# Two attention stages and the last scatters of a four-layer model: DRAM row for the spread, products for the last group, adds into the output

## The reference, cut to what matters

```python
# L1 and L3 attention, per head of 64 columns
attn = softmax(q @ k.T * scale)        # 1024 queries; 1024 + 154 keys
out  = (attn @ v) @ Wo + bo

# L3 feed-forward: 32 experts, 4 chosen of each of 2048 tokens, 320 places in each expert
buf_tok = full(E * cap + 1, N).at[dest].set(tok)     # a free place holds the token number N
out = einsum(silu(xe @ w1) * (xe @ w3), w2) * buf_w
y = zeros((N + 1, DIM)).at[buf_tok].add(out)[:N]     # what falls on row N is dropped
return y + z                                         # z is a shared expert
```

## Time and profile before

| | us |
|---|---|
| median of 3 runs | 3202.24 (3200.54 to 3202.68) |
| the profiled execution's own time | 3204.76 |
| its span, first to last instruction | 3203.0 |
| PE busy in the span | 2851.1 (89%) |
| DVE busy | 1890.4 (59%) |
| ACT busy | 1432.0 (45%) |
| POOL busy | 586.9 (18%) |

### The profile page before, as it was taken

How to read it: one execution, slowest core, us unless ns; L and a number is a source line. 1 busy time by engine, 2 the same in 40 slices (tenths; PEclk the granted TensorE clock), 3 DMA queues, 4 the chain that set the end, 5 groups by cost and what they waited for, 6 DMA issues and landing times. The chain is left out here.

```text
span 3203.0 us, 46363 instructions
## 1 busy us (share of the span) xinstructions
PE 2851.1 (89%) x13988; PEld 2126.9 (66%) x13989; DVE 1890.4 (59%) x3602; ACT 1432.0 (45%) x2987; POOL 586.9 (18%) x655
## 2 busy tenths in 40 slices
PE   5796779986997989999689999999999999968996
PEld 4795545546886779999456666666666666646665
DVE  4414465516555354443588888878788888664443
ACT  1233544431211224544347766767676777711111
POOL 0133010001442200000200000000000000106776
PEclk8698879996999779999799999999999999979999
DMA  1342022223232010000112323233222332335776
GB/s 40 107 163 92 1 32 23 22 11 117 84 103 81 13 40 27 26 13 1 24 25 24 31 22 31 22 33 31 31 21 30 23 31 22 13 72 149 162 173 144
DMA packets 153723, 168.84 MB, mean 53 GB/s; under 512 B 38128, under 2 KB 123014, under 8 KB 153286
## 3 DMA queue, kind: packets, MB, share of 16 engines
q1 hardware_dynamic: 115878, 105.16, 20.2%
q0 software_dynamic: 21280, 37.93, 5.5%
q10 hardware_dynamic: 16416, 24.12, 2.3%
HBM read 105.77 MB, written 29.84 MB: 42 GB/s over the span
## 5 line engine op out<-in xcount | busy, mean ns | idle before, releaser
L2036 ACT ACTIVATE l3a_pt_hi<-l3a_banks 128x512 fp32r<-128x512 f32 (+2 forms) x640 | 382.9, 598 | 326.6 <-PE l3a_banks L1977 272.4
L2147 DVE TENSOR_TENSOR l3a_pt_lo<-l3a_pt,l3a_pt_hi 128x512 fp32r<-128x512 f32 (+2 forms) x640 | 459.9, 727 | 75.9 <-ACT l3a_pt L2037 38.8
L2037 ACT ACTIVATE l3a_pt<-l3a_banks 128x512 f32<-128x512 f32 (+2 forms) x640 | 378.7, 592 | 0.0
L2117 DVE TENSOR_REDUCE l3a_maxima<-l3a_banks 128x1 f32<-128x1178 f32 x256 | 351.5, 1375 | 3.5 <-PE l3a_banks L1924 3.3
L2182 POOL TENSOR_TENSOR l3a_out_t<-l3a_out,l3a_shared 64x512 f32<-64x512 f32 x65 | 90.3, 1390 | 1134.2 <-DMA l3a_shared<-l3a_inverse 1134.2
L1977 PE MATMUL l3a_banks<-l3a_pt_hi,l3a_v 128*65 128x512 f32 (+2 forms) x640 | 287.7, 449 | 6.1 <-ACT l3a_out L2051 3.8
L1990 PE MATMUL l3a_banks<-l3a_q,l3a_k 128*128 128x512 f32 (+2 forms) x640 | 253.9, 397 | 13.0 <-ACT l3a_pt L2037 11.4
L1991 PE MATMUL l3a_banks<-l3a_q,l3a_k 72*128 72x512 f32 (+5 forms) x640 | 252.8, 395 | 0.0
L1977 PE MATMUL l3a_banks<-l3a_pt_lo,l3a_v 128*65 128x512 f32 (+2 forms) x640 | 251.9, 394 | 0.0
L1977 PE MATMUL l3a_banks<-l3a_pt_hi,l3a_v_lo 128*65 128x512 f32 (+2 forms) x640 | 251.8, 393 | 0.0
L1924 PE MATMUL l3a_banks<-l3a_k,l3a_q 128*128 128x512 f32 (+1 forms) x768 | 207.3, 378 | 16.0 <-DVE l3a_maxima L2117 16.0
(11 more groups left out here) (583 smaller groups left out, 5876.7 us busy)
## 6 DMA issues: line engine op xcount, KB each, us to landing
l3f_w<-in_L_ffn_w SPq DMA_DIRECT2D x96, 256.0 KB, 3.7
l0f_w<-in_L_ffn_W ACTq DMA_DIRECT2D x12, 1024.0 KB, 6.5
l1f_w<-in_L_ffn_W ACTq DMA_DIRECT2D x18, 512.0 KB, 4.6
l3a_shared<-l3a_inverse SPq DMA_DIRECT2D x65, 128.0 KB, 6.3
l2f_w<-in_L_ffn_w SPq DMA_DIRECT2D x16, 512.0 KB, 4.5
l3a_q<-l3a_q SPq DMA_DIRECT2D x64, 128.0 KB, 2.3
l3a_k<-l3a_k SPq DMA_DIRECT2D x64, 128.0 KB, 2.3
l0f_w<-in_L_ffn_W SPq DMA_DIRECT2D x4, 1024.0 KB, 7.2
```

Of the source, the lines that this page charges most:

```text
L2036: act.activation(a.pt_hi[0:rows, n % a.pt_slots, :], a.st_bank[0:rows, n % 2, :], ACT.Exp, bias=bias, scale=scale)
L2037: act.activation(a.pt[0:rows, n % 4, :], a.st_bank[0:rows, n % 2, :], ACT.Exp, bias=bias, scale=scale).then_inc(a.exped, 1)
L2117: dve.tensor_reduce(a.maxima[:, n:n + 1], banks.rearrange("p a b -> p (a b)")[:, 0:KEYS], AX.X, ALU.max).then_inc(a.maxed, 1)
L2147: dve.tensor_tensor(a.pt_lo[0:rows, slot, :], a.pt[0:rows, n % 4, :], a.pt_hi[0:rows, slot, :].bitcast(F32), ALU.subtract).then_inc(a.lo_m ...
```

## The change

- `inverse` is no longer a row in SBUF but a DRAM tensor of 512 floats. The inverted totals are written to it (128 partitions with 16 bytes each), and the spread reads it 64 times from DRAM.
- The last group of the last unit no longer goes over SP and POOL. PE turns its row of totals by four products with one row and one column ("tr": 1x128 by 1x1) into 128x4; DVE inverts them, multiplies them with the identity matrix into `diagonal` (128 x 512); one product with ones ("ts": 128x128 by 128x512, float32) puts every inverted total on every partition; DVE multiplies `out` with it out of PSUM into `out_t`. Then "e4" to "e7" follow as before.
- The scatters of the last feed-forward part add to the output tensor itself, with a bound: indices over 2047 are dropped. The rows of zeros behind the tokens and the copy at the end are gone.

```diff
-        self.inverse = sb("inverse", [1, BLOCK])
+        self.inverse = nc.dram_tensor("l3a_inverse" if projected else "l1a_inverse", [1, BLOCK], F32, kind="Internal").ap()
+        self.diagonal, self.last_totals = sb("diagonal", [P, BLOCK]), sb("last_totals", [P, BLOCK // P])
@@ side_pe
+    elif name == "tr":
+        pe.wait_ge(a.o_kept, number(unit, GROUPS - 1) + 1)
+        for n in range(BLOCK // P):
+            ins = pe.matmul(bank[:, n:n + 1], a.out[HEAD:HEAD + 1, 1, n * P:(n + 1) * P], chip.ones[HEAD:HEAD + 1, 0:1], start=True, stop=True)
+    elif name == "ts":
+        pe.wait_ge(a.diagonal_made, 1)
+        ins = pe.matmul(bank[:], chip.ones[:], a.diagonal[:], start=True, stop=True)
...
-            pe.wait_ge(a.ot_done, number(unit, 1 if t == 0 else 3) + 3)
+            pe.wait_ge(a.ot_done, number(unit, 1 if t == 0 else 2) + 3)
+            if t == 4:
+                pe.wait_ge(a.side_read[uses.bank("ts")], uses.read_with("ts"))
@@ move_totals
-    sp.dma_start(a.inverse[:], a.totals[:]).then_inc(a.returned, 16)
+    sp.dma_start(a.inverse.rearrange("a (p n) -> (a p) n", p=P), a.totals[:]).then_inc(a.returned, 16)
     sp.wait_ge(a.returned, k * 16 + 16)
-    sp.dma_start(a.shared[:, g % 2, :], a.inverse[:].unsqueeze(1).to_broadcast([1, HEAD, BLOCK])).then_inc(a.spread_out[g % 2], 16)
+    sp.dma_start(a.shared[:, g % 2, :], a.inverse.rearrange("a n -> (a n)").partition_broadcast(HEAD)).then_inc(a.spread_out[g % 2], 16)
@@ in place of attention_end
+def attention_end_pe(pe, chip, a, last, project):
+    for name in ("tr", "ts", *OWN_LAST):
+        side_pe(pe, chip, a, a.epilogue(last), name, last, 1, project)
+
+def attention_end_dve(dve, chip, a, last):
+    uses = a.epilogue(last)
+    dve.wait_ge(a.side_done, uses.done_with("tr"))
+    dve.reciprocal(a.last_totals[:], a.side[:, uses.bank("tr"), 0:BLOCK // P]).then_inc(a.side_read[uses.bank("tr")], 1)
+    dve.wait_ge(a.side_read[uses.bank("tr")], uses.read_with("tr"))
+    dve.tensor_tensor(a.diagonal[:].rearrange("p (n q) -> p n q", q=P), chip.ident[:].unsqueeze(1).to_broadcast([P, BLOCK // P, P]),
+                      spread(a.last_totals[:], P), ALU.mult).then_inc(a.diagonal_made, 1)
+    hi, _ = head_rows(1)
+    dve.wait_ge(a.side_done, uses.done_with("ts"))
+    dve.tensor_tensor(a.out_t[hi, 1, BLOCK:2 * BLOCK], a.out[0:HEAD, 1, :], a.side[0:HEAD, uses.bank("ts"), :], ALU.mult
+                      ).then_inc(a.side_read[uses.bank("ts")], 1)
+    for name in OWN_LAST:
+        add_output(dve, chip, a, uses, name, 1)
@@ l3_ffn
-    sums = nc.dram_tensor("l3f_sums", [TOKENS + PIECE_COLUMNS * P, D], F32, kind="Internal").ap()
+    sums = out.rearrange("b s d -> (b s) d")
...
-            sp.dma_start(sums[TOKENS:, :].rearrange("(j p) d -> p j d", p=P), empty[:, :, 0:D]).then_inc(based, 16)
...
             sp.wait_ge(summed, 48 * E)
-            for b in range(BATCH):
-                sp.dma_start(out[b], sums[b * SEQ:(b + 1) * SEQ, :]).then_inc(copied, 16)
-            sp.wait_ge(copied, 16 * BATCH)
+            sp.sem_inc(copied, 1)
...
-            pool.wait_ge(based, 32)
+            pool.wait_ge(based, 16)
...
                     pool.indirect_dma_start(sums, bass.IndirectOffsetOnAxis(token_index[0:n, u, j:j + 1], 0), y_rows[0:n, u, j, :], None,
-                                            compute_op=ALU.add).then_inc(summed, 16)
+                                            bounds_check=TOKENS - 1, oob_is_err=False, compute_op=ALU.add).then_inc(summed, 16)
```

More of the change, by code:

```diff
@@ L1773, with __init__ @@
 class Attention:
-    def __init__(self, sb, psum, sem, projected, gate, split=False, out_t=None):
+    def __init__(self, nc, sb, psum, sem, projected, gate, split=False, out_t=None):
         self.gate, self.split = gate, split
@@ L1813, in __init__ @@
         self.spread_out = [sem("spread_out0"), sem("spread_out1")]
-        self.passed_pe = sem("passed_pe")
+        self.passed_pe, self.last_inverted, self.diagonal_made = sem("passed_pe"), sem("last_inverted"), sem("diagonal_made")
         self.parts = Q_PARTS + V_PARTS if projected else ()
@@ L1834, in epilogue @@
         done, read = self.uses_before(unit)
-        return Uses(list(OWN_LAST), done + 13, read, len(self.first_order) + 13, 0)
+        return Uses(["tr", "ts", *OWN_LAST], done + 13, read, len(self.first_order) + 13, 0)
 class Projection:
@@ L2520, in l1_attention @@
             sb, psum, sem = scope(nc, stack, "l1a2")
-            a = Attention(sb, psum, sem, projected=False, gate=chip.gates[:, 1:2],
+            a = Attention(nc, sb, psum, sem, projected=False, gate=chip.gates[:, 1:2],
                                   out_t=chip.xn[:, 0:8, :].rearrange("p (u t) d -> p u (t d)", u=2))
@@ L2575, in _ @@
                     pe, chip, a, unit, u, uses_of(unit, following), project, mask, following))
-                last = BATCH * PAIRS - 1
-                for name in OWN_LAST:
-                    side_pe(pe, chip, a, a.epilogue(last), name, last, 1, project)
+                attention_end_pe(pe, chip, a, BATCH * PAIRS - 1, project)
             @block.scalar
@@ L2594, in _ @@
                     dve, chip, a, unit, u, uses_of(unit, following), project, following))
-                attention_end(None, dve, None, a, BATCH * PAIRS - 1)
-                for name in OWN_LAST:
-                    add_output(dve, chip, a, a.epilogue(BATCH * PAIRS - 1), name, 1)
+                attention_end_dve(dve, chip, a, BATCH * PAIRS - 1)
             @block.gpsimd
@@ L2625, in l3_attention @@
         gb = sb("gb", [P, D])
-        a = Attention(sb, psum, sem, projected=True, gate=chip.gates[:, 3:4], split=True)
+        a = Attention(nc, sb, psum, sem, projected=True, gate=chip.gates[:, 3:4], split=True)
         turn = TurnSemaphores(sem, "t")
@@ L2705, in _ @@
             cycle(BATCH * PAIRS - 1, 1, False, None)
-            attention_end(sp, None, None, a, BATCH * PAIRS - 1)
         @block.tensor
```

3 lines of the change are left out of this document (removed).

## The result

Four runs of the changed kernel gave a median of 3152.8 us, where the kernel before has 3202.4; one of the four was disturbed (11020 us) and is left out of the ratio, and the other three have a median of 3150.0. The ratio is 0.984 (95% interval 0.982 to 0.986). The profiled execution took 3155.6 us with a span of 3153.9, against 3204.8 and 3203.0.

The account below looks back on a forecast made before the run. PE, busy for 89%, was taken as the bound, with POOL nearly full in the expert loop and serial chains at the ends. Savings of 16.0 + 7.4 + 8.4 + 0 = 31.8 us gave 3170.4 us (median), range 3158 to 3188.

Parts of the forecast that it names:

- The ends: Ends of layer 1's and layer 3's attention: new chain of 4.8 us each, 16.0 us saved in all (13 to 19).
- the clock's 1.0: Both attention ends: with PE idle for shorter times its products may run at 2.4 GHz; 0.5 us each, 1.0 in all.
- The steady units: Layer 3 attention's running units: DVE's wait for totals goes, saving PE 0.5 us in 14 units, 0.4 in the last; 7.4.
- The collision with POOL: Layer 3's running units: POOL's earlier scaling meets DVE's subtraction, costing DVE 1.2 us and PE 0 to 0.3.
- The copy: Kernel's end: the copy to the output goes with SP's whole wait, 8.4 us saved; the 1.5 us behind it stay.
- Rival 4: Kernel's end: the last scatter lands slowly in the output tensor, so the wait moves; 3170 plus at most 4 us; chance 0.03.
- The scatters: Expert loop: the bound on 96 scatters gives 0 us, with +0.58 and -0.58 us per scatter as limits.

Follow-up runs that it names:

- a1: The changed kernel run once more without any edit; 3157.8 us, 0.985 of the kernel before.
- e4: The kernel before with only the bound added to the last layer's 96 scatters; 3203.0 us, ratio 1.000.
- e9: The kernel before, spreads from SBUF, with layer 3's group 2 spread issued behind the second part of the next unit's q; 3180.9 us, ratio 0.993.
- f1: The changed kernel with group 2's spread moved behind the turn and a 128 KB SBUF transfer nobody reads in its old place; 3173.2 us, 0.991 of the kernel before.
- e10: The changed kernel with layer 3's group 2 spread issued behind the turn of the loop's body; 3150.2 us, 0.984 of the kernel before.

## Why the prediction was wrong

- **The ends: right.** Forecast 16.0 with the clock's 1.0, measured 7.6 + 7.9 = 15.5 in the two chains. The chain was 4.87 and 4.19 us for 4.8. The 1.0 for the clock did not come, as "e4" ran at 1.2 GHz; that the sum still came within 0.5 us is in part luck, as layer 1's chain was 0.6 us shorter than forecast.
- **The steady units: mechanism right, size off.** "0.5 saved in 14 units, 7.0, and 0.4 in the last" measured 18.3 in 15 units and nothing in the last. The failed step is "1.87 us of DVE cost PE 0.79; the other 1.08 were slack". It read the first place where PE was late and took the rest for absorbed. DVE has next to no slack from there on: between the wait and the second place it stands idle only once for more than 0.1 us, for 0.14. Aligned on slot 12, PE's instructions of the two traces lie 0.7 us apart from 13.1 us on, 1.2 from 26 on and 1.3 from 39 on. The second place, in the same unit, stood in the old trace:

```profile
2205.66 0.60 PE L1896 MATMUL l3a_side<-l3a_wo,l3a_out_t 128*128 128x256 f32 x2
2206.47 0.74 PE L1924 MATMUL l3a_banks<-l3a_k,l3a_q 128*128 128x512 f32 x2 [0.21 <-DVE l3a_maxima L2117]
```

  0.81 us lie between these starts, where an undelayed pair has 0.24, in the trace after too. The 29 waits of the earlier trace rows were two for each of 14 units (and one at the start), not one, which the count alone would have told. The collision with POOL came (L2157 took 1.49 us twice behind slot 12) and cost PE nothing; the 0.3 taken off for it was too much. The Trainium skill ("SBUF — State Buffer", section "Who interferes with whom") has the two instructions take turns; the 1.49 us agree with it, but its price did not reach PE.
- **The turns of the loop: not seen.** This is the second step that failed, and the larger one: the sum has no term for them. The changed stages gained 53.8 us, 22.0 more than the sum: 10.9 of it in the units, 13.9 at the turns, less 3.0 at the copy. Of the 13.9 some 5.1 are the clock, which fell behind two turns in place of five. In a second trace of the changed kernel (a1) it fell behind four, and the turns gave 9.1, so this term is partly chance. The row "issue: 30.4, 5" was in a view that the prediction used. I left a row without a releaser alone, and priced the shorter spread only by who waits for its data. With it the question would have been which transfer lies over those five moments.
- **The copy: cause wrong in part.** "All of that goes: 8.4 us" and "the 1.5 us behind it stay" held SP's chain for the only one. Below it lay GpSimd's DRAIN, which had ended 5.3 us earlier (3196.2 and 3201.5) and now sets the end. From the last scatter's landing to the last instruction are 5.1 us (a1: 3158.2 to 3163.3) where 1.5 to 2 were forecast. Rival 4 came nearest, a wait that moves, though not in the output tensor.
- **The scatters: right.** The bound is free (e4), and the loop has not moved: POOL 94.9 of 120 us where the earlier trace rows had 94.4, and PE's wait for gathered rows is 21.8 us in 18 times for 22.4 in 19.

```profile
2886.00:3006.00 120.00, 109.28 (x469) 79.58 (x468) 49.97 (x142) 17.05 (x49) 94.86 (x72) 0.99 0.64 153
```

```profile
PE l3f_p_xt L3025 <- DMA l3f_x_rows<-l3f_rows,l3f_in_index: 21.8, 18, 1.9
```

The range was too narrow for the same reason as the centre: its lower end assumed that all that could be won was already on the list.

## What to carry to other kernels

When a wait of a nearly full engine goes, do not price it at the first place where the bound engine is late: count the waits per unit, and line up a whole unit. A row "<- issue" with few, long, regular occurrences is a question that needs an answer before the forecast; here it was code held back by a transfer, and moving the transfer behind the loop's turn takes the loss from 5.3 to 1.1 us a turn without making the transfer shorter (e9). When a stand of the bound engine varies from turn to turn, look at the granted clock behind it before looking for a second cause. When the last piece of a chain is taken away, look at what every engine does at the block's end, the queues' DRAIN included.

## What the runs showed of the hardware

- Reading 2 KB of one SBUF row 64 times into 64 partitions takes 6.3 us from issue to landing, the same from a row in DRAM 3.2 us; the write of the row took 1.4 us to DRAM and 1.9 us to SBUF.
- Such a transfer lasts 4.8 us from its first to its last packet. In 4.2 us of it no packet of the instruction queue moved (before, f1); at a turn of the loop's body VectorE stood 6.1 us, 4.0 of it with its input there (before), and ScalarE 5.8 (f1). A turn cost 5.3 us (before) and up to 7.5 (f1), against 1.0 to 1.4 with no such transfer beside it (e9, e10).
- Behind a turn the granted clock of TensorE stood at 1.2 GHz for 3.4 us in all five turns before, in two of the changed kernel and in none of e10; turns with it cost 1.7 us more than turns without (3.7 and 2.0 us).
- GpSimd's DRAIN at the end of a block ended 4.9 us behind its last indirect scatter in five traces, whatever else ran.
- Bounds on an indirect scatter with addition cost nothing: 1.577 us in the median with and without.
